# Cross-attention and a ternary feed-forward layer: where the softmax exponential is taken

## The reference

```python
def xattn(q, kv, Wq, Wk, Wv, Wo):                 # q = layernorm(x), kv = ctx
    qh, kh, vh = (rope'd) q @ Wq, kv @ Wk, kv @ Wv   # 16 query heads in 4 groups, 4 kv heads, 32 wide
    scores = einsum('bghsd,bhad->bhsa', qh, kh)      # the groups are summed
    attn = softmax(scores / 32 ** 0.5, axis=-1)      # over the 77 rows of the context
    out = einsum('bhsa,bhad->bhsd', attn, vh).mean(heads)
    return out @ Wo

x = x + xattn(layernorm(x), ctx, Wq, Wk, Wv, Wo)
h = layernorm(x)                                   # then a quantised layer
i_scale = max(abs(h)) / 127                        # over the whole tensor
x = x + clip(round(h / i_scale)) @ ternary(weight).T * w_scale * i_scale + bias
```

## Time and profile before

| | |
|---|---|
| median of 3 runs | 1320.01 us (1319.31 to 1321.22) |
| the profiled execution | 1319.5 us |
| its span, from first to last instruction | 1317.7 us |
| attention steps, roughly | from 150 to 930 us of the span |
| costliest group on ACT in the attention | L691, 161.4 us in 256 |
| the exponentials, L667 | 129.2 us in 256 |
| the subtractions, L944, on DVE | 108.9 us in 256 |
| maxima, L940, on DVE | 110.1 us in 256 |

### The profile page before, as it was taken

How to read it: one execution, slowest core, us unless ns; L and a number is a source line. 1 busy time by engine, 2 the same in 40 slices (tenths; PEclk the granted TensorE clock), 3 DMA queues, 4 the chain that set the end, 5 groups by cost and what they waited for, 6 DMA issues and landing times.

```text
span 1317.7 us, 36811 instructions
## 1 busy us (share of the span) xinstructions
PE 1267.9 (96%) x9848; PEld 1085.9 (82%) x9911; DVE 1181.8 (90%) x2772; ACT 1025.1 (78%) x2338; POOL 791.2 (60%) x1536
## 2 busy tenths in 40 slices
PE   5897999999999999999999999999969999999998
PEld 5796999999999999999999999999935555555554
DVE  4876899999999999999999999999978888888887
ACT  3454788888888888888888888888857878888886
POOL 3564888888888888888888888888820000000000
PEclk9999999999999999999999999999979999999999
DMA  8574355555555555555546452323108999999945
GB/s 266 166 216 133 107 158 182 154 183 161 176 165 171 165 171 167 170 171 166 178 159 187 150 169 76 102 80 98 37 5 332 400 401 395 401 399 404 406 201 223
DMA packets 100815, 265.18 MB, mean 201 GB/s; under 512 B 49705, under 2 KB 65769, under 8 KB 72114
## 3 DMA queue, kind: packets, MB, share of 16 engines
q1 hardware_dynamic: 100786, 264.86, 58.8%
HBM read 139.64 MB, written 125.17 MB: 201 GB/s over the span
## 4 chain that ended last, share of the span: by engine, by line
DVE 47%; PE 31%; issue 15%; DMA 2%; DVEq 2%; SPq 1%; ACT 1%; POOL 1%; POOLq 0%; ACTq 0%
PE bank L1248 18%; DVE amax L898 10%; DVE x_sb L930 8%; DVE e_sb L944 6%; DVE mx_sb L940 5%; DVE bn_sb L889 5%; PE bank L1239 4%; PE bank L1246 3%; DVE qT_sb L912 2%; PE bank L1065 2%; DVE rinv_sb L886 2%; DVE ve_sb L918 2%; DVE bn_sb L881 2%; DVE mv_sb L904 1%; DMA x_sb<-in_ctx 1%
## 5 line engine op out<-in xcount | busy, mean ns | idle before, releaser
L1248 PE MATMUL bank<-wT,x_sb 128*128 128x512 f16 x1024 | 263.9, 380 | 3.5 <-issue 0.2
L1168 PE MATMUL bank<-wqs,xT_sb 128*128 128x128 f32 x2048 | 259.7, 280 | 0.2
L718 ACT ACTIVATE x_sb<-bank,mean,cols 128x512 f32<-128x512 f32 x256 | 196.0, 774 | 67.6 <-PE bank L1248 67.3
L1168 PEld LDWEIGHTS bank<-wqs,xT_sb 128*128 128x128 f32 x2048 | 238.2, 191 | 7.1 <-ACT xT_sb L640 0.8
L1216 PE MATMUL bank<-v_blk,pT_sb 103*128 103x136 f32 x1536 | 199.0, 279 | 0.3 <-ACT pT_sb L682 0.3
L1216 PEld LDWEIGHTS bank<-v_blk,pT_sb 103*128 103x128 f32 x1536 | 190.6, 190 | 0.5 <-ACT pT_sb L682 0.5
L1248 PEld LDWEIGHTS bank<-wT,x_sb 128*128 128x128 f16 x1024 | 100.5, 98 | 106.8 <-issue 1.6
L930 DVE SCALAR_TENSOR_TENSOR x_sb<-x_sb,negm,bank 128x512 f32 (+1 forms) x256 | 179.5, 742 | 7.9 <-PE bank L1179 2.7
L898 DVE TENSOR_REDUCE amax<-x_sb (+1 forms) x128 | 156.0, 1218 | 23.2 <-DVE bn_sb L889 8.0
L691 ACT ACTIVATE sq_sb<-x_sb 128x512 bf16 (+1 forms) x256 | 161.4, 631 | 18.7 <-DVE x_sb L930 1.4
L1005 DVE TENSOR_TENSOR x_sb<-x_sb 128x512 f32 (+1 forms) x256 | 164.5, 683 | 1.2 <-ACT x_sb L718 1.2
(11 more groups left out here) (126 smaller groups left out, 2584.4 us busy)
## 6 DMA issues: line engine op xcount, KB each, us to landing
out_y<-x_sb SPq DMA_DIRECT2D x112, 1024.0 KB, 7.2
x_sb<-in_x SPq DMA_DIRECT2D x64, 1024.0 KB, 6.5
x_sb<-out_y SPq DMA_DIRECT2D x48, 1024.0 KB, 9.0
x_sb<-in_ctx SPq DMA_DIRECT2D x38, 256.0 KB, 2.8
k_blk<-k_scr SPq DMA_DIRECT2D x256, 19.2 KB, 5.5
k_scr<-x_sb SPq DMA_DIRECT2D x38, 128.0 KB, 2.3
v_scr<-x_sb SPq DMA_DIRECT2D x38, 68.0 KB, 2.3
v_blk<-v_scr SPq DMA_DIRECT2D x128, 10.2 KB
```

The lines of the kernel that those rows point to most:

```text
L718: act.activation(u_sb[:, t, :], bank[4 + t][:, :], ACT.Identity, bias=stat_of(mean1, j, t, back), scale=cols[:, 6:7]).then_inc(scaled_t, 1)
L1168: last = pe.matmul(bank[2][:, t * HD:(t + 1) * HD], xT_sb[:, t, c, :], wqs[:, c, :], start=c == 0, stop=c == EC - 1)
L1248: last = pe.matmul(bank[4 + t][:, :], q16T_sb[:, t, c, :], wT[:, c, :], start=False, stop=c == EC - 1)
```

## The change

The exponential of L667 goes. The instruction that copies the transposed scores out of their bank (L682), so far a plain copy, takes the exponential. As a row of x lies along the free axis there, the row scale can no longer be a scale per partition of the activation: it is applied before the transposes, in the subtraction on DVE, which becomes `rs * score - rs * max` (one scalar_tensor_tensor for each tile). For that the maxima of both tiles are multiplied by `rs` in one small instruction between the maxima and the subtractions. PE's transposes wait for the subtraction (`sub_done_t`) instead of the exponential.

```diff
+        mxs_sb = sb("mxs_sb", [P, 2, HEADS])
@@ ACT, step
-                if value:
-                    j, kj, gj = value
-                    act.wait_ge(rs_ready, j + 1)
-                    for t in range(2):
-                        act.wait_ge(sub_done_t, 2 * j + t + 1)
-                        act.activation(e_sb[:, kj % 2, t, :], e_sb[:, kj % 2, t, :], ACT.Exp,
-                                       scale=rs_sb[:, kj, t:t + 1]).then_inc(exp_done_t, 1)
...
                         act.activation(pT_sb[0:CR, t, :], bank[6 + t][0:CR, 0:CHUNKS * P],
-                                       ACT.Copy).then_inc(pT_copied_t, 1)
+                                       ACT.Exp).then_inc(pT_copied_t, 1)
@@ DVE, step
                     for t in range(2):
                         dve.tensor_reduce(mx_sb[:, t, :], bank[4 + t][:, 0:SC].rearrange("p (h a) -> p h a", h=HEADS),
                                           AX.X, ALU.max).then_inc(mx_ready, 1)
-                    for t in range(2):
-                        dve.wait_ge(mx_ready, 2 * j + t + 1)
-                        dve.tensor_tensor(e_sb[:, kj % 2, t, :].rearrange("p (h a) -> p h a", h=HEADS),
-                                          bank[4 + t][:, 0:SC].rearrange("p (h a) -> p h a", h=HEADS),
-                                          mx_sb[:, t, :].unsqueeze(2).broadcast_to([P, HEADS, CTX]),
-                                          ALU.subtract).then_inc(sub_done_t, 1)
+                    dve.wait_ge(rs_ready, j + 1)
+                    dve.wait_ge(mx_ready, 2 * j + 2)
+                    dve.tensor_tensor(mxs_sb[:, :, :], mx_sb[:, :, :],
+                                      rs_sb[:, kj, :].unsqueeze(2).broadcast_to([P, 2, HEADS]),
+                                      ALU.mult).then_inc(mxs_ready, 1)
+                    dve.wait_ge(mxs_ready, j + 1)
+                    for t in range(2):
+                        dve.scalar_tensor_tensor(out=e_sb[:, kj % 2, t, :].rearrange("p (h a) -> p h a", h=HEADS),
+                                                 in0=bank[4 + t][:, 0:SC].rearrange("p (h a) -> p h a", h=HEADS),
+                                                 scalar=rs_sb[:, kj, t:t + 1],
+                                                 in1=mxs_sb[:, t, :].unsqueeze(2).broadcast_to([P, HEADS, CTX]),
+                                                 op0=ALU.mult, op1=ALU.subtract).then_inc(sub_done_t, 1)
@@ PE, step
-                    pe.wait_ge(exp_done_t, 2 * j + 2)
+                    pe.wait_ge(sub_done_t, 2 * j + 2)
```

More of the change, by code:

```diff
@@ L247, in build @@
             sem(n) for n in ("rope_mul", "qr_ready", "qT_done", "qT_copied"))
-        sc_done_t, mx_ready, sub_done_t, exp_done_t = (
-            sem(n) for n in ("sc_done_t", "mx_ready", "sub_done_t", "exp_done_t"))
+        sc_done_t, mx_ready, sub_done_t, mxs_ready = (
+            sem(n) for n in ("sc_done_t", "mx_ready", "sub_done_t", "mxs_ready"))
         pT_done_t, pT_copied_t, pv_done, pv_copied = (
```

## The result

| | time (us) | against the kernel before |
|---|---|---|
| before | 1320.62 | |
| changed | 1404.71 (1403.38 to 1405.31) | 1.0643 (1.0624 to 1.0662) |
| predicted | 1350 (1334 to 1366) | |

The change costs 84 us. The forecast had the sign, and the engine that becomes the bound, but less than half of the size.

What follows compares the result with a forecast made beforehand. PE was taken to bound the kernel at 6.55 us a step; DVE's 6.37 + 0.30 (multiplication and drains) + 0.12 (subtractions) = 6.79 makes DVE the bound, and 122 steps x 0.245 = 30 us give 1350 us, range 1334 to 1366.

Steps and rivals of the forecast that it cites:

- the sign: Whole kernel: the change makes it slower, by more than 2.6 us; chance 0.91.
- PE's 6.55: Attention steps: PE has no gap and needs 6.55 us a step.
- DVE has a reserve: Attention steps: DVE needs 6.37 us a step by itself, so 0.18 us more a step is free.
- who becomes the bound: Attention steps after the change: DVE, at 6.79 us a step against PE's 6.55.
- where PE waits: In front of the scores (L1203), PE waits for DVE's low part of q (L912).
- The exponentials are worth nothing on ACT, and cost nothing at the copy: ACT, L667 and L682: removing 1.01 us a step gains nothing; exponentials in the copies cost 0, or 0.14 without cover.
- scalar_tensor_tensor 0.06 more each: DVE's two subtractions: the new form costs 0.06 us more each, +0.12 a step; bounds 0 and 0.28 each.
- I take 0.16: DVE's small multiplication between maxima and subtractions: lasts 0.16 us, between 0.07 and 0.18.
- The wait in front of it: DVE, from the second maximum's end to the multiplication's start: 0.035 us.
- rival 1: Same mechanism, other sizes: 1335 with old subtraction costs, 1377 with 0.14 per dependent step on DVE; chance 0.07 each.
- The wait behind it: DVE, from the multiplication's end to the first subtraction's start: 0.035 us.
- Rival 2: Semaphores cost DVE nothing, the multiplication only 0.07: DVE at 6.56 a step, 1320 to 1325 us; chance 0.06.

Runs made afterwards that it cites:

- Run 3: Changed kernel without the small multiplication of the maxima by the row scale; the scalar_tensor_tensor subtract the plain maximum: 1318.3 us, 0.9987.
- Run 5: Kernel before plus one lone 128x8 DVE multiplication a step, two SBUF operands, no waits, result unread, behind both maxima: 1328.3 us, 1.0063.
- run 1: Changed kernel with the maxima in a free part of bank 4 instead of SBUF, so the multiplication reads one bank operand: 1353.1 us, 1.0248.
- run 4: Run 3 with the subtraction of the kernel before and no row scale, so only the exponential moves: 1318.8 us, 0.9991.
- run 2: Changed kernel with the second rope product and the addition left out on POOL, so POOL is idle at the multiplication: 1351.0 us, 1.0238.
- run 7: Changed kernel, full arithmetic; maxima, means, variances in banks 4 and 5, statistics' aggregations and tensor_scalar moved around the multiplication to fill drains: 1326.0 us, 1.0044.
- run 9: Changed kernel with POOL's rope addition made in two halves of 128x128: 1371.6 us, 1.0400.
- Run 6: Changed kernel with the small multiplication split in two tensor_scalar of 128x4, row scale as scalar per partition: 1423.1 us, 1.0778.
- run 12: Changed kernel without the maxima's multiplication, first tile's e_sb transposes before PE's projection, means and variances in bank 5, statistics instructions moved: 1321.0 us, 1.0005.

## Why the prediction was wrong

- **PE's 6.55, that DVE has a reserve, who becomes the bound, where PE waits:** right. Run 3 adds 0.12 a step to DVE and costs nothing.
- **The size of the reserve:** between 0.18 and about 0.24. Run 5 adds 0.26 in the mean and costs 8 us, where 0.18 would give (0.26 - 0.18) x 122 = 10; but there only two steps in five pay. In run 1 and in the changed kernel DVE is the bound in every step, and its own need can be read back. Run 1's step is 6.83; from the second maximum to the first subtraction it has 0.78 for 0.39, in the two subtractions 0.13 more. That leaves 6.83 - 0.39 - 0.13 = 6.31, and the changed kernel, 7.25 - 0.81 - 0.13, the same: by this estimate a reserve of 0.24, and 0.06 a step, 7 us, too much in the forecast's sum.
- **The exponentials are worth nothing on ACT, and cost nothing at the copy:** right (run 4). The copies' line on the page of the changed kernel (busy time, mean ns of one, idle time before them):

```profile
L675 ACT ACTIVATE pT_sb<-bank 103x384 f32<-103x384 f32 x256 | 111.6, 488 | 53.5 <-PE bank L1188 53.5
```

  488 ns with the exponential, 489 as a plain copy. ACT's busy time fell by 111 us, not 129: the two instructions had overlapped their neighbours.
- **scalar_tensor_tensor 0.06 more each:** right, 0.45 from start to start for 0.39 (runs 1 and 3).
- **The step that failed: "I take 0.16" for the multiplication**, with the bounds 0.07 and 0.18. The instruction by itself is 0.167 (runs 1 and 2), but it lasts 0.61, because it reads two SBUF operands while POOL is in the middle of an instruction. I took both bounds from DVE's own rows and never laid POOL's beside them. 0.45 x 122 = 55 us by the sum, 52 by run 1. Without it the changed kernel is at 1353, 3 us from the forecast; that it is so near is partly luck if the reserve is the larger one, for then it and the wait below err by 7 and 8 us in opposite directions.
- **The wait in front of it:** 0.035 was taken, 0.10 measured (492.10 to 492.20, and as much in run 1), on the way to the 0.14 of rival 1 and with its argument: of the two semaphores in front, one is waited for in an instruction of its own (the chain of the trace has it at 492.14, L936). 0.07 x 122 = 8 us. The wait behind it, 0.04, was as taken.
- **Rival 2**, that semaphores cost DVE nothing, falls: with the wait for POOL gone, run 1 is still 33 us above the kernel before. Filled drains (run 7, with the semaphores still there) bring most of that back, so it is the drains, not the semaphores as such. Not all of the 27 us between the two runs is theirs: the first tensor_scalar of the statistics also takes 0.08 of the queue there instead of 0.19, since it reads a bank. In this trace a dependent instruction starts 0.035 after the end of the one before, where independent neighbours overlap by 0.07 to 0.08. So what that section of the Trainium skill ("VectorE: DVE Perf Modes", "The DRAIN you can't avoid") measured, that semaphores between chained operations cost nothing extra, doesn't hold here. For the emptying of the pipe the section names an exception itself, a next operation that isn't held starts earlier; the prediction left it out.

The sign could be read before. L918 and L920 are two tensor_scalar of 128x2 on the same tile, L918 with a multiplication and an addition, L920 with a multiplication alone. In DVE's timeline of the kernel before, with POOL's row beside it:

```profile
489.32 0.30 DVE L918 TENSOR_SCALAR ve_sb<-mv_sb 128x2 f32<-128x2 f32 x1
489.53 0.15 DVE L920 TENSOR_SCALAR negm<-mv_sb 128x2 f32<-128x2 f32 x1
```

```profile
489.18 0.41 POOL L530 TENSOR_TENSOR ost_sb<-pw_sb 128x128 fp32r<-128x128 f32 x1
```

One lasts twice the other, and ends at 489.62, 0.03 after POOL's 489.59. The added operation isn't the reason: L875, the same form with both operations, lasts 0.15 at 486.16, and POOL is idle there, from 485.63 to 486.50. So equal instructions of unequal length were there, and I took a short one, L875, as the row for a small instruction.

The Trainium skill has the rule ("SBUF — State Buffer", section "Who interferes with whom"): VectorE and GpSimd share a pair of SBUF ports as an exclusive lock for a whole instruction, and a VectorE instruction with two SBUF inputs contends with a GpSimd instruction that reads SBUF, while one with at most one SBUF input outside the two-port modes doesn't; tensor_scalar can enter such a mode. Run 1 agrees (0.17 with one SBUF operand, POOL at work), and so do the changed kernel (0.61 with two) and run 9 (the multiplication ends with the one POOL instruction in progress). Run 6 agrees if its tensor_scalar was in a two-port mode, which no row shows.

## What to carry to other kernels

Before a small instruction is put on a vector engine's critical stretch, lay the rows of GpSimd at that moment beside it: if both of its tensor operands lie in SBUF, or if it is a tensor_scalar on an SBUF tensor as in run 6, its price can be what is left of GpSimd's instruction (here 0.45 us for 8 elements). With an operand in a matmul bank instead it was not there (runs 1, 7 and 12). Then count the drains that it opens, and look for independent work to stand in them; look also what the moved work stood in front of (run 7). If equal instructions have unequal lengths in the trace, find out why before one of them is used as a price.

## What the runs showed of the hardware that was not expected

- Even a tensor_scalar of 128x4 with one SBUF tensor operand waits for POOL's instruction (0.62 us, run 6). The tensor_scalar of the statistics, 0.30 out of SBUF, takes 0.15 when it reads from a bank (run 12).
- It is phase that decides: 0.01 us ahead of POOL's addition the lone multiplication passes in 0.16, 0.13 behind it takes 0.63 (run 5). So a change of a tenth of a microsecond elsewhere on DVE can cost or give back half a microsecond a step.
- Splitting POOL's instruction in two, which makes POOL's work longer, gave back 33 us of the 84 (run 9).
